# A gated cross-attention and NVFP4 feed-forward kernel: the fourth sequence's attention from gathered rows, its later stages one step on, and a new order of the set-up

## What is computed

```
x = x + tanh(g_xattn[0]) * xattn(layernorm(x), ctx, router, W_q, b_q, token_to_sets)
x = x + tanh(g_ffn[0])   * ffn(layernorm(x), gate, up, down weights in 4-bit codes with scales)

xattn: scores = (layernorm(x) W_q^T + b_q) router^T / 16      # 64 sets, only the token's 4 allowed ones
       top 2 of them, softmax over the two, weighted sum of the two rows of ctx
ffn:   out = (gelu_tanh(x Wg^T) * (x Wu^T)) Wd^T              # 256 -> 2048 -> 256
```

## Time and profile before

| | |
|---|---|
| median of 3 runs | 311.27 us (311.02 to 311.34) |
| the profiled execution, its own time | 311.26 us |
| its span in the trace | 309.5 us |
| granted TensorE clock | full (2.4 GHz) over nearly the whole span |
| busy: PE, PEld, DVE, ACT, POOL | 302.0, 251.0, 223.6, 155.9, 144.8 us |

### The profile page before, as it was taken

One profiled execution on the slowest core, in us unless ns is written; L12 is line 12 of the kernel. 1 busy time (PEld: TensorE's weight loads), 2 busy tenths in 40 slices (PEclk: granted clock), 3 DMA queues, 4 the chain that ended last, 5 costly groups with the idle time before them and its releaser, 6 DMA issues.

```text
span 309.5 us, 4648 instructions
## 1 busy us (share of the span) xinstructions
PE 302.0 (98%) x1537; PEld 251.0 (81%) x1537; DVE 223.6 (72%) x478; ACT 155.9 (50%) x287; POOL 144.8 (47%) x138
## 2 busy tenths in 40 slices
PE   6998999999999999999999999999999999999996
PEld 4777888787788788888888888888888888888885
DVE  3999999899985669687676678777676565544545
ACT  3476665657455453435555453444654533444341
POOL 3447455636742342876353325866442233432421
PEclk9999999999999999999999999999999999999999
DMA  6970440020000021326240111424130001110102
GB/s 184 253 186 0 150 124 0 0 37 1 0 2 0 2 34 17 77 57 123 70 101 3 17 17 26 94 53 85 63 94 0 0 15 26 26 40 0 37 0 68
DMA packets 47288, 16.11 MB, mean 52 GB/s; under 512 B 38944, under 2 KB 44448, under 8 KB 47264
## 3 DMA queue, kind: packets, MB, share of 16 engines
q1 hardware_dynamic: 44576, 12.92, 18.0%
q0 software_dynamic: 864, 2.10, 2.5%
q10 hardware_dynamic: 1824, 0.79, 1.1%
HBM read 11.08 MB, written 3.15 MB: 46 GB/s over the span
## 4 chain that ended last, share of the span: by engine, by line
PE 78%; issue 7%; POOL 6%; DVE 4%; ACT 2%; DMA 2%; SPq 0%; DVEq 0%; POOLq 0%
PE ring_ps L1317 49%; PE acc_ps L1351 17%; PE acc_ps L1364 4%; PE att_ps L1364 3%; POOL act_lo L525 3%; POOL w_nat L507 2%; DMA x_sb<-in_x_dram 2%; PE att_ps L1219 1%; POOL w_nat L518 1%; PE ring_ps L1302 1%; ACT act L695 1%; DVE act L1006 0%; DVE act L1000 0%; DVE x_sb L1157 0%; ACT act L691 0%
## 5 line engine op out<-in xcount | busy, mean ns | idle before, releaser
L525 POOL TENSOR_TENSOR act_lo<-act,act_hi 128x512 fp32r<-128x512 f32 x63 | 82.1, 1302 | 118.8 <-ACT act_hi L702 118.6
L1317 PE MATMUL ring_ps<-xt_hi,w_hi 128*128 128x512 f32 (+1 forms) x264 | 103.8, 394 | 1.0 <-ACT xt_hi L675 0.7
L1317 PE MATMUL ring_ps<-xt_hi,w_lo 128*128 128x512 f32 (+1 forms) x264 | 100.9, 384 | 0.0
L1317 PE MATMUL ring_ps<-xt_lo,w_hi 128*128 128x512 f32 (+1 forms) x264 | 100.2, 384 | 0.0
L691 ACT ACTIVATE act<-ring_ps 128x512 f32<-128x512 f32 x64 | 38.1, 596 | 84.2 <-PE ring_ps L1317 83.8
L1000 DVE SCALAR_TENSOR_TENSOR act<-act,ring_ps 128x512 f32<-128x512 f32 x64 | 43.7, 683 | 39.1 <-ACT act L691 38.9
L1006 DVE SCALAR_TENSOR_TENSOR act<-act,ring_ps 128x512 f32<-128x512 f32 x64 | 43.8, 685 | 27.2 <-ACT act L695 25.9
L1317 PEld LDWEIGHTS ring_ps<-xt_hi,w_hi 128*128 128x128 f32 x264 | 49.7, 188 | 11.1 <-issue 1.2
L1317 PEld LDWEIGHTS ring_ps<-xt_lo,w_hi 128*128 128x128 f32 x264 | 49.0, 188 | 10.3 <-DVE xt_lo L938 0.2
L695 ACT ACTIVATE act<-act 128x512 f32<-128x512 f32 x64 | 40.5, 632 | 32.7 <-DVE act L1000 32.7
L1317 PEld LDWEIGHTS ring_ps<-xt_hi,w_lo 128*128 128x128 f32 x264 | 49.8, 188 | 8.3
(11 more groups left out here) (129 smaller groups left out, 331.9 us busy)
## 6 DMA issues: line engine op xcount, KB each, us to landing
x_t<-in_x_dram SPq DMA_DIRECT2D x48, 32.0 KB, 2.1
w_nat<-w_nat SPq DMA_DIRECT2D x96, 16.0 KB
out_dram<-x_sb SPq DMA_DIRECT2D x6, 256.0 KB, 2.2
x_sb<-in_x_dram SPq DMA_DIRECT2D x1, 1024.0 KB, 8.4
ln_dram<-normed SPq DMA_DIRECT2D x16, 64.0 KB, 2.2
w_nat<-ln_dram SPq DMA_DIRECT2D x16, 64.0 KB, 2.0
packed<-L_ffn_gate_W_packed_dram SPq DMA_DIRECT2D x3, 256.0 KB, 2.9
packed<-n_L_ffn_up_W_packed_dram SPq DMA_DIRECT2D x3, 256.0 KB, 3.3
```

The costliest lines, as they stand in the source:

```text
L525: pool.tensor_tensor(act_lo[:, s % RING, :], act[:, s % ACT_RING, :], act_hi[:, s % RING, :].bitcast(F32), ALU.subtract).then_inc(inter_lo, 1)
L1317: i = pe.matmul(into[:, tok], wt[:, n, w], xt[:, c % 2, k, tok], start=(k, j) == order[0], stop=(k, j) == order[-1])
```

## The change

`BY_ROWS` goes from 4 to 3, so that sequence 3 gets its attention by gathered rows, as sequences 4 to 7 do. In `FIRST_STEPS` its add moves from step 12 to step 13; center stays at 14. In `LATER_STEPS` attend moves to the step of weigh, one step earlier, for both sequences. In the set-up calls are put in another order on four engines, and score of sequence 2 moves from behind down(0) to ahead of gate(2). The load of the context rows on SP carries one sequence instead of two for the second chunk.

```diff
-    FIRST_STEPS = ((None, None, 2, 3, 5, 6, 7, 9, 10, 10), (7, 8, 8, 9, 10, 11, 12, 14, 15, 15))
-    LATER_STEPS = ((0, 0, 1, 2, 3, 4, 6, 8, 12, 12), (3, 3, 4, 5, 6, 7, 9, 11, 15, 15))
-    BY_ROWS = 2 * CB
+    FIRST_STEPS = ((None, None, 2, 3, 5, 6, 7, 9, 10, 10), (7, 8, 8, 9, 10, 11, 13, 14, 15, 15))
+    LATER_STEPS = ((0, 0, 1, 2, 3, 3, 6, 8, 12, 12), (3, 3, 4, 5, 6, 6, 9, 11, 15, 15))
+    BY_ROWS = CB + 1
...
             x_t_out(1)
+            compact(0)
             lead_out(0)
-            compact(0)
...
+            compact(1)
             probs_out(0)
             lead_out(1)
+            rows_high(0)
+            normalise(0)
             sc.wait_ge(down_scales_loaded, 16)
...
             attend_first(1)
...
+            turn_tile(2)
+            first_products("gate", 0)
+            first_products("up", 0)
+            first_products("gate", 1)
             turn_normed(1)
...
+            first_products("up", 1)
+            second_products("gate", 0, gate_done)
+            turn_tile(3)
             turn_tile(4)
+            second_products("up", 0, up_done)
+            second_products("gate", 1, gate_done)
+            second_products("up", 1, up_done)
+            score(CB)
```

More of the change, by code:

```diff
@@ L557, in _ @@
             root_2(1)
-            for i in range(2):
-                scale_rows_of(1, i)
+            scale_rows_of(1, 0)
+            scale_rows_of(1, 1)
+            root_1(CB)
             scale_down_of(1)
-            root_1(CB)
-            for i in range(2):
-                scale_rows_of(2, i)
+            scale_rows_of(2, 0)
+            scale_rows_of(2, 1)
             for c in range(CHUNKS):
@@ L724, in _ @@
                           ACT.Copy).then_inc(down_scales_placed, 1)
-            compact(1)
-            rows_high(0)
-            normalise(0)
             probs_out(1)
@@ L740, in _ @@
             square(1)
+            rows_high(3)
             tanh(1)
-            rows_high(3)
             for c in range(CHUNKS):
@@ L1046, in _ @@
             find_where(0)
+            unpack(0, 0)
             weigh(0)
             input_variance(1)
-            for stage in range(3):
-                unpack(0, stage)
+            unpack(0, 1)
+            unpack(0, 2)
             read_scores(1)
             find_top(1)
-            find_lead(1)
             update_stats(0)
             update_variance(0)
+            find_lead(1)
             find_where(1)
@@ L1058, in _ @@
             weigh(1)
+            unpack(1, 0)
             rows_low(0)
-            unpack(1, 0)
             unpack(1, 1)
@@ L1067, in _ @@
             unpack(1, 2)
-            down_tile_low(0)
             turn_blocks(CB)
             input_stats(CB)
+            down_tile_low(0)
             ln2_low(1)
+            unpack(2, 0)
             input_variance(CB)
-            for stage in range(3):
-                unpack(2, stage)
+            unpack(2, 1)
             cubic(0)
             rows_low(2)
+            unpack(2, 2)
             gated_of(0)
@@ L1080, in _ @@
             gated_of(1)
+            inter_of(1)
             rows_low(3)
-            inter_of(1)
             for c in range(CHUNKS):
@@ L1319, in project, with first_products, second_products @@
                 return i
+            def first_products(kind, u):
+                if kind == "gate":
+                    pe.wait_ge(rows_lo, u + 1)
+                bank_free(kind, u)
+                project(0, u, ("gate", "up").index(kind), bank_of(kind, u), slice(0, ST), 1)
+            def second_products(kind, u, done):
+                project(0, u, ("gate", "up").index(kind), bank_of(kind, u), slice(ST, TOK), 2).then_inc(done, 1)
             def gate(s):
@@ L1401, in _ @@
             score(1)
+            turn_probs(0)
             warm(2)
-            turn_probs(0)
             warm(4)
             attend_first(0)
+            warm(4)
             add_x(1)
@@ L1409, in _ @@
             turn_tile(1)
-            warm(4)
             turn_probs(1)
@@ L1450, in _ @@
                     for b in next_sequences(c, n, SCORE):
-                        score(b)
+                        if b > CB:
+                            score(b)
                     for b in next_sequences(c, n, ATTEND):
```

## The result

The changed kernel takes **315.33 us** (median of 4 runs, 314.98 to 315.43); the kernel before took 311.14 us beside it (311.0 to 311.34). The ratio is 1.0132, with a 95% interval of 1.0115 to 1.015: slower by about 4.1 us. The prediction said slower, at 312.5 us, with a range that ended at 313.5. The span grew from 309.5 to 313.6 us, as much as the time.

What follows compares the result with a forecast made beforehand. TensorE, busy 98% of the 309.5 us span, was taken to bound the kernel. Gate(16) later by 1.7 us and the set-up shorter by 0.4 us gave +1.3 us on 311.27, so 312.5 us; range 310.7 to 313.5.

Steps and rivals of the forecast that it cites:

- The rest: Later chunks' one-step earlier gathers on GpSimd: costed at 0, uncovered up to 0.9 us in each of two chunks; smaller context load: 0.
- The cover of two steps: Later chunks: TensorE needs the results of a step with moved gathers only two steps on, so their cost is 0.
- The set-up: Stretch up to gate(3): moving score(2) ahead of gate(2) wins 0.4 us, bounds 0 and 1.0 us, limited by VectorE.
- Step 11: First chunk: attention of sequence 3 leaves TensorE and wins 0.85 us, between 0.35 and 1.01 us.
- The later chain of sequence 3: First chunk, gathers to gate(16): late additions delay normalise(3), TensorE waits, and gate(16) moves by +1.7 us, step 11's gain included.
- Both holds: First addition of sequence 3 on VectorE: waits for gathered rows to land and for GpSimd's low_part(12); 93.7 with both.
- The loss by order on ScalarE: First chunk: normalise(3) stands ahead of square(14), so gated(14) is late and TensorE loses 1.0 us at up(15).
- part is won: Rival: VectorE moves further ahead in steps 11 to 13, set-up gives 1.0 us, half the stall stays: 310.5 us, chance 0.08.

## Why the prediction was wrong

- **The step that failed is "The rest".** It costed the one-step earlier gathers of the later chunks at 0, since TensorE needs the results of such a step two steps on, and named 0.9 us in each of two chunks as the price without that cover, for a late root_2. Measured, that table costs 3.2 us (by the ratio) to 3.6 us (by the traces), 1.8 us in each of two chunks. The range ended 1.8 us under the measured time, and this term is larger than that. The step followed what comes behind the gathers on GpSimd only as far as root_2. In between stand the output addition and the low part, and the prediction's own fact of the earlier trace rows, that a small VectorE instruction waits for a GpSimd one beside it, was used in the first chunk and not here. The cover of two steps was overrun as well: one addition in step 6 took 3.35 us instead of 0.48, and the 2.9 us reached gate(25), three steps on.
- **The set-up** was put at 0.4 us, and the run with it alone gives 0.4 us (interval from 0.8 won to 0.1 lost). So the size is not contradicted, but the agreement is partly luck: the reading under it, that VectorE worked through the set-up without a pause, is wrong. In the trace before it stands idle for 2.77 us up to 3.75 and 0.96 us up to 5.98, both for loads. The traces' 0.84 us would have misled: one of them was late.
- **Step 11** was put at 0.85 us and is 0.86: gate(11) to gate(12) went from 5.91 to 5.06 us. The estimate that VectorE's loss of three instructions brings the low half of tile 19 forward held.
- **The later chain of sequence 3** was right in its mechanism and nearly in size. On the clock of the trace before, with the 0.84 us of that trace's set-up added, the additions end at 94.7 (94.8 predicted), normalise ends at 98.0 (98.2), gate(15) is at 98.2 (98.5), up(15) at 100.6 (100.9), gate(16) at 103.6 (103.8). Both holds that it named for the first addition came: 0.37 us of idle for the landing, and then 0.82 instead of 0.48 us beside low_part(12). These are the rows of DVE and ACT of the changed kernel:

```profile
91.86 2.01 DVE L892 SCALAR_TENSOR_TENSOR x_sb<-choice,row_weights,x_sb 128x256 f32<-128x256 f32 x4 [0.37 <-DMA choice<-in_ctx_dram,rows_at]
...
95.79 0.16 DVE L925 SCALAR_TENSOR_TENSOR shift<-moments,rstd 128x2 f32<-128x2 f32 x1 [0.84 <-POOL rstd L491]
```

```profile
95.99 1.13 ACT L667 ACTIVATE normed<-x_sb,shift,rstd 128x256 f32<-128x256 f32 x2 [3.48 <-DVE shift L925]
97.02 0.58 ACT L691 ACTIVATE act<-ring_ps 128x512 f32<-128x512 f32 x1
```

- **The loss by order on ScalarE** (up(15), 1.0 us predicted) was 0.78 us of waiting, and the run with square(14) first gave 0.85 us back.
- **The rivals**: none had the later chunks in it, so the range, made from their cases, could not hold the time. The rival *part is won* has a slip in its sum: 1.85 us won against 1.3 lost is 310.7 us and not 310.5; nothing hangs on it. The sum of the prediction for sequence 3 and the set-up, +1.3 us, stands beside +1.2 us measured for the kernel with the old later table.

## What to carry to other kernels

- A step that is moved by one number moves everything behind it on its queue. List what stands behind it there up to the next wait, and hold each instruction against the other engines' timeline; the cheap looking number put 2.3 us of gathers in front of two tensor instructions.
- Where two engines exclude each other, half a microsecond decides who is first, and the loser waits until the other's instruction is over (1.04 us of a low part here). Such places need slack in both directions, and a small delay upstream comes out larger there.
- Size a set-up's gain by several executions and not by one profile.

## What the runs showed of the hardware

- A VectorE addition of 0.48 us with two SBUF inputs took 1.52 us with one GpSimd tensor instruction beside it that had begun 0.26 us earlier. The other way round GpSimd's low part took 1.49 us instead of 1.30 where it began 0.14 us behind the addition. The Trainium skill, page "SBUF — State Buffer", section "Who interferes with whom", says that whichever issues first keeps the shared ports for its whole instruction; the trace agrees in these two cases.
- Beside two GpSimd tensor instructions back to back (135.98 to 138.51) such an addition took 3.35 us, in six of six places (two each in the changed kernel, in the one with the later table alone and in the one with its second number alone). That is no rule for every pair. In the trace of the kernel before, L863 (two SBUF inputs, 128x256 like the additions) began beside a scaling on GpSimd that ended at 50.47 with the low part right behind it. L863 ended 0.28 us after the scaling, and it was the low part that took longer (1.48 us instead of 1.29):

```profile
49.95 0.80 DVE L863 TENSOR_TENSOR choice<-iota_i,top_at 128x256 f32<-128x256 int32 x1
```

```profile
50.43 1.48 POOL L525 TENSOR_TENSOR act_lo<-act,act_hi 128x512 fp32r<-128x512 f32 x1
```

Nor does the order of the starts explain the 3.35 us, as the addition's record begins 0.53 us ahead of the first of the pair, while a gather was still running. Whether a gather with a tensor instruction right behind it is what does it, no run here shows.
- A VectorE instruction with a single SBUF tensor as input was held too: the variance of 2 elements at L920 took 1.26 us beside the low part, and 0.17 us alone. The bn_stats instructions before it were not: both began beside a low part in the kernel with the old table and took 0.42 and 0.41 us. The same section of the Trainium skill's page names tensor_scalar among the operations that can take both port pairs, so that agrees as well.
- Two indirect gathers beside the same additions held them by no more than 0.06 us in four (1.73 against 1.67 us). One of the two gathers took 1.19 us there, where the other gathers of that trace take 0.94 to 1.10, all but its like in the next chunk (1.20).
